# Relative attention: score blocks of 32 queries by four heads, with rounded and remainder query parts stacked

## The reference, cut to what matters

```python
rk2, rv2 = rel_k[idx], rel_v[idx]
attn1 = jnp.einsum('bhqd,bhkd->bhqk', rq, rk)
attn2 = jnp.einsum('bhqd,qkd->bhqk', rq, rk2)
attn = jax.nn.softmax((attn1 + attn2) * (1.0 / math.sqrt(c)), axis=-1)
w1 = jnp.einsum('bhqk,bhkd->bhqd', attn, rv)
w2 = jnp.einsum('bhqk,qkd->bhqd', attn, rv2)
```

## Time and profile before

| | |
|---|---|
| three runs, median (lowest to highest) | 1922.81 us (1922.19 to 1923.03) |
| span of the profiled execution | 1922.3 us, 59270 instructions; its own time around the span is not recorded apart from the runs |
| PE busy in the span | 1656.3 us (86%) |
| VectorE, ScalarE, GpSimd busy | 1402.0 (73%), 938.9 (49%), 882.1 (46%) us |

### The profile page before, as it was taken

One profiled execution on the slowest core, in us unless ns is written; L12 is line 12 of the kernel. 1 busy time (PEld: TensorE's weight loads), 2 busy tenths in 40 slices (PEclk: granted clock), 3 DMA queues, 4 the chain that ended last, 5 costly groups with the idle time before them and its releaser, 6 DMA issues. The chain is left out here.

```text
span 1922.3 us, 59270 instructions
## 1 busy us (share of the span) xinstructions
PE 1656.3 (86%) x21927; PEld 1392.3 (72%) x21927; DVE 1402.0 (73%) x3369; ACT 938.9 (49%) x2305; POOL 882.1 (46%) x1710
## 2 busy tenths in 40 slices
PE   5999999999979884999599999999999999648750
PEld 4888888888858773999478888888888888525430
DVE  6777777877758884666787888888888888635434
ACT  2222212221228770677467777777777777424320
POOL 3333333333202566566232455445555555547771
PEclk9999999999989995999699999999999999869985
DMA  8900000000022001222323333333333333256537
GB/s 298 165 0 0 0 0 0 0 0 0 0 81 102 23 25 55 65 72 65 124 60 63 74 87 78 77 77 78 76 79 80 86 77 78 63 149 171 169 102 271
DMA packets 312667, 147.60 MB, mean 77 GB/s; under 512 B 205238, under 2 KB 291284, under 8 KB 312020
## 3 DMA queue, kind: packets, MB, share of 16 engines
q1 hardware_dynamic: 299876, 118.38, 25.3%
q0 software_dynamic: 12544, 25.91, 3.9%
HBM read 72.03 MB, written 73.37 MB: 76 GB/s over the span
## 5 line engine op out<-in xcount | busy, mean ns | idle before, releaser
L2143 POOL DMA_INDIRECT x_slots<-rel_x,rel_at x128 | 135.5, 1059 | 212.5 <-PE rel_s_ps L1727 186.9
L535 PE MATMUL tok_main_ps<-tok_w_h,tok_feat_h 128*128 128x512 f32 x512 | 205.3, 401 | 0.9 <-DVE tok_feat_low L99 0.9
L1966 ACT ACTIVATE rel_e<-rel_s_ps,rel_neg_max 128x255 f32<-128x255 f32 x512 | 200.2, 482 | 10.7 <-DVE rel_neg_max L2299 9.5
L535 PE MATMUL tok_main_ps<-tok_w_h,tok_feat_l 128*128 128x512 f32 x512 | 200.6, 392 | 0.0
L535 PE MATMUL tok_main_ps<-tok_w_l,tok_feat_h 128*128 128x512 f32 x512 | 200.3, 391 | 0.0
L2299 DVE TENSOR_REDUCE rel_neg_max<-rel_s_ps 128x4 f32<-128x1020 f32 x128 | 155.9, 1218 | 53.2 <-PE rel_s_ps L1727 51.2
L84 POOL TENSOR_TENSOR tok_q_pre<-tok_v_q,tok_v 128x128 f32 (+1 forms) x32 | 39.0, 1219 | 310.5 <-DVE tok_q L274 295.8
L1707 PE MATMUL rel_s_ps<-rel_k_h,rel_q_head_h 128*128 128x256 f32 x512 | 154.6, 302 | 0.2 <-DVE rel_q_head_l L2273 0.2
L1748 PE MATMUL rel_t_ps<-all_k_ident,rel_e 128*128 128x128 f32 x1024 | 139.3, 279 | 14.4 <-issue 14.0
L294 DVE TENSOR_TENSOR tok_prod<-tok_main_ps,tok_v 128x1024 f32<-128x1024 f32 x64 | 78.4, 1225 | 97.9 <-PE tok_main_ps L540 97.9
L1748 PEld LDWEIGHTS rel_t_ps<-all_k_ident,rel_e 128*128 128x128 f32 x1024 | 109.6, 141 | 47.0 <-issue 45.8
(11 more groups left out here) (406 smaller groups left out, 4725.2 us busy)
## 6 DMA issues: line engine op xcount, KB each, us to landing
rel_q_rep<-q_rows SPq DMA_DIRECT2D x256, 64.0 KB, 2.5
o_rows<-rel_rv SPq DMA_DIRECT2D x256, 64.0 KB
x_slots<-early_zeros SPq DMA_DIRECT2D x16, 520.0 KB, 6.2
exp_x<-x_slots SPq DMA_DIRECT2D x32, 260.0 KB, 3.0
y_rows<-early_zeros SPq DMA_DIRECT2D x16, 512.0 KB, 5.8
final_y<-y_rows SPq DMA_DIRECT2D x16, 512.0 KB, 12.0
exp_x<-x_slots SPq DMA_DIRECT2D x72, 65.0 KB, 1.9
q_rows<-rel_qT SPq DMA_DIRECT2D x64, 64.0 KB
```

Source lines behind the costliest of these rows:

```text
L535: nc.tensor.matmul(main_ps[s][:, cols], feat[fk][:, s, j, :], w_p[wk][:, j, cols], start=(j == 0 and (fk, wk) == (0, 0)), stop=False)
L1966: last = nc.scalar.activation(e[u % 2][:, n, 0:L], s_ps[u % 2][:, n, 0:L], ACT.Exp, bias=neg_max[u % 2][:, n:n + 1])
L2143: nc.gpsimd.indirect_dma_start(x1_slots[:], bass.IndirectOffsetOnAxis(ap=at[n][:, k, t:t + 1], axis=0), x1[n][:, t, k, :], None).then_inc( ...
```

## The change

A block of scores becomes 32 queries by four heads. The rounded and the remainder part of a query are stacked along the contraction: four heads by two parts by 16 channels are 128 rows. The key weights and query weights are laid out with each head's channels twice, in two halves a of four heads, so one projection becomes two matmuls. `content` then needs two matmuls per block, one with rounded keys and one with key remainders; the loop puts all rounded-key products of a unit first. The position part takes eight queries by 16 channels as its 128 rows and 32 columns (four heads by eight queries); its table window follows the eight queries. The queries are loaded from DRAM straight into a zeroed `q_pos`, in sixteen loads instead of eight, and `position_queries`, `round_queries`, `queries_rest` and `queries_remainder` are replaced by `split_queries`, one subtraction per head pair and half. The transposed exponentials are copied into `eT` in runs of sixteen, so that `positions` and `values` find a quad's eight heads together.

```diff
-def table_keys(blk):
-    if blk < NBLK // 2:
-        return 0, min(L, BQ * blk + BQ + MAX_REL - 1)
-    return max(0, BQ * blk - MAX_REL + 1), L
+def table_keys(u, q0):
+    if u < NU // 2:
+        return 0, min(L, q0 + OCT + MAX_REL - 1)
+    return max(0, q0 - MAX_REL + 1), L
 def attention_weights(bench, w):
...
-        x, xT, qT = m.sb("x", [P, 2, D]), m.sb("xT", [P, T]), m.sb("qT", [P, T])
+        x, xT, qT = m.sb("x", [P, 2, D]), m.sb("xT", [P, T]), m.sb("qT", [P, 2, OCT, T // OCT])
...
-        q_head = [[m.sb(f"q_head{r}_{k}", [P, T // QUAD, H, QUAD], FP32R) for k in "hl"] for r in range(2)]
-        eT = [m.sb(f"eT{s}", [P, 2, NBLK // 2, P]) for s in range(2)]
-        q_hl = m.sb("q_hl", [P, 2, 2, T], FP32R)
-        q_scale, q_bias, set_up = m.sb("q_scale", [P, 2]), m.sb("q_bias", [P, 2]), m.sem("set_up")
-        q_rep = m.sb("q_rep", [P, H, T // 2])
-        q_pos = [m.sb(f"q_pos{r}", [P, T // (2 * QUAD), H, QUAD]) for r in range(2)]
+        q_head = [[m.sb(f"q_head{r}_{a}", [P, T // OCT, 2, H // 2, QUAD], FP32R) for a in range(2)] for r in range(2)]
+        eT = [m.sb(f"eT{s}", [P, 2, 4, 4, 2, 2, P // 8]) for s in range(2)]
+        q_round = m.sb("q_round", [P, 2, OCT, T // OCT], FP32R)
+        q_scale, q_bias, set_up = m.sb("q_scale", [P, 1]), m.sb("q_bias", [P, 2]), m.sem("set_up")
+        q_pos = [m.sb(f"q_pos{r}", [P, 2, 2, H // 2, QUAD, T // OCT]) for r in range(2)]
...
-        def of_heads(q, k):
-            return q[32 * k:32 * k + 32, :, 2 * k:2 * k + 2, :]
-        def of_pair(part, k):
-            return q_hl[32 * k:32 * k + 32, part].rearrange("p o (g i) -> p g o i", i=QUAD)
-        def keys_for(k, u):
-            return k[:, int(u < NU // 2), :]
+        def by_octets(ap):
+            return ap.rearrange("p (g i) -> p i g", i=OCT)
+        def of_head(ap, a, k):
+            return ap[32 * k:32 * k + 32, a].rearrange("p (w i) g -> p g w i", w=2)
+        def in_blocks(ap):
+            return ap.rearrange("p (a q) (c w k) -> p a (q c w) k", a=2, c=4, w=2)
+        def turned_blocks(eT_t, u):
+            return eT_t[:, 2 * (u % 2):2 * (u % 2) + 2].rearrange("p q c w a k -> p a (q c w) k")
...
                 def repeat_queries(b, r):
...
-                    for f in range(2):
-                        sp.dma_start(q_rows[r][:, f], qT[:].rearrange("p (u f t) -> p u f t", f=2, u=NU)[:, :, f])\
-                            .then_inc(q_out, 16)
-                    sp.wait_ge(q_out, 32 * b + 32)
-                    if after(b, 1):
-                        sp.wait_ge(qp_ready, b)
-                    for f in range(2):
-                        for i in range(QUAD):
-                            at = 64 * f + HD * i
-                            sp.dma_start(q_rep[at:at + HD],
-                                         q_rows[r][:, f].rearrange("(h d) u t -> d h (u t)", d=HD)).then_inc(q_in, 16)
+                    if after(b, 2):
+                        sp.wait_ge(s_done, NU * (b - 1))
+                    sp.dma_start(q_rows[r], qT[:]).then_inc(q_out, 16)
+                    sp.wait_ge(q_out, 16 * b + 16)
+                    if b == 0:
+                        sp.wait_ge(zeroed, 6)
+                    for i in range(OCT):
+                        for a in range(2):
+                            sp.dma_start(q_pos[r][HD * i:HD * i + HD, a, i // QUAD, :, i % QUAD, :],
+                                         q_rows[r].rearrange("(h v d) a i g -> d h v a i g", v=2, d=HD)[:, :, 0, a, i, :])\
+                                .then_inc(q_in, 16)
...
                 def project_k(b):
...
-                    nc.tensor.matmul(pa, wk_sb[:], xT[:], start=True, stop=True).then_inc(k_done, 1)
+                    for a in range(2):
+                        last = nc.tensor.matmul(pa_halves[:, a, :], wk_sb[:, a * P:(a + 1) * P], xT[:], start=True, stop=True)
+                    last.then_inc(k_done, 1)
                 def project_q(b):
...
-                    nc.tensor.matmul(pa, wq_sb[:], xT[:], start=True, stop=True).then_inc(q_done, 1)
+                    for a in range(2):
+                        last = nc.tensor.matmul(pa_halves[:, a, :], wq_sb[:, a * P:(a + 1) * P], xT[:], start=True, stop=True)
+                    last.then_inc(q_done, 1)
...
                 def content(b, u, r):
...
-                        pe.wait_ge(qh_ready, 4 * b + 4)
-                        pe.wait_ge(ql_ready, 4 * b + 4)
-                    for n in range(UB):
-                        blk = UB * u + n
-                        for qk, kk in THREE:
-                            nc.tensor.matmul(s_ps[u % 2][:, n, :],
-                                             q_head[r][qk][:, 4 * blk:4 * blk + 4].rearrange("p c h i -> p (c h i)"),
-                                             keys_for(k_p[r][kk], u),
-                                             start=((qk, kk) == (0, 0) and n % 2 == 0), stop=False,
-                                             skip_group_check=True)
+                        pe.wait_ge(q_split, 2 * b + 2)
+                    for k in range(2):
+                        for q in range(2):
+                            g = 4 * (2 * u + q)
+                            for a in range(2):
+                                nc.tensor.matmul(s_ps[u % 2][:, 2 * a + q, :],
+                                                 q_head[r][a][:, g:g + 4].rearrange("p c w h i -> p (c w h i)"),
+                                                 k_p[r][k][:, a, :], start=(k == 0 and q == 0), stop=False,
+                                                 skip_group_check=True)
                 def position_scores(b, u, r):
...
-                        pe.wait_ge(tables_made, 3)
+                        pe.wait_ge(tables_made, 2)
...
-                        pe.wait_ge(qp_ready, b + 1)
+                        pe.wait_ge(q_in, 16 * 2 * OCT * (b + 1))
...
-                    for k in range(2):
-                        for f in range(2):
-                            n = 2 * f + k
-                            lo, hi = table_keys(UB * u + n)
+                    for q in range(2):
+                        for a in range(2):
...
-                                off = KOFF - BQ * (UB * u + n) - QUAD * c
+                                g = 4 * (2 * u + q) + c
+                                lo, hi = table_keys(u, OCT * g)
+                                off = KOFF - OCT * g
...
-                                    s_ps[u % 2][32 * c:32 * c + 32, n, lo:hi],
-                                    q_pos[r][64 * f:64 * f + 64, 8 * u + 4 * k + c].rearrange("p h i -> p (h i)"),
-                                    table[64 * f:64 * f + 64, off + lo:off + hi], start=False, stop=True,
-                                    skip_group_check=True)
+                                    s_ps[u % 2][32 * c:32 * c + 32, 2 * a + q, lo:hi],
+                                    q_pos[r][:, a, :, :, :, g].rearrange("p w h i -> p (w h i)"),
+                                    table[:, off + lo:off + hi], start=False, stop=True, skip_group_check=True)
                 def turn_e(b, u):
...
-                    if b == 0:
-                        act.wait_ge(tables_made, 1)
-                    for end in range(2):
-                        last = nc.scalar.activation(k_p[r][0][:, end], pa, ACT.Identity, bias=bk_end[:, end:end + 1])
+                    act.wait_ge(set_up, 2)
+                    for a in range(2):
+                        last = nc.scalar.activation(k_p[r][0][:, a], pa_halves[:, a], ACT.Identity, bias=bk_sb[:, a:a + 1])
                 def read_q(b):
...
-                        act.wait_ge(q_out, 32 * b)
-                        act.wait_ge(rest_ready, b)
-                        act.wait_ge(qh_ready, 4 * b)
-                    else:
-                        act.wait_ge(set_up, 2)
-                    for odd in range(2):
-                        nc.scalar.activation(q_hl[:, 0, odd], pa, ACT.Identity, bias=q_bias[:, odd:odd + 1],
-                                             scale=q_scale[:, odd:odd + 1])
-                    nc.scalar.activation(qT[:], pa, ACT.Identity, bias=bq_sb[:], scale=SCALE).then_inc(q_ready, 1)
-                def round_queries(b, r, pairs):
-                    act.wait_ge(q_ready, b + 1)
-                    if after(b, 2):
-                        act.wait_ge(s_done, NU * (b - 1))
-                    act.wait_ge(set_up, 2)
-                    for k in pairs:
-                        nc.scalar.activation(of_heads(q_head[r][0], k), of_pair(0, k).bitcast(FP32), ACT.Copy)\
-                            .then_inc(qh_ready, 1)
+                        act.wait_ge(q_out, 16 * b)
+                        act.wait_ge(q_split, 2 * b)
+                    for a in range(2):
+                        nc.scalar.activation(q_round[:, a], by_octets(pa_halves[:, a]), ACT.Identity, bias=q_bias[:, a:a + 1],
+                                             scale=q_scale[:])
+                    for a in range(2):
```

(56 more changed lines are left out.)

71 lines of the change are left out of this document (31 added, 40 removed).

## The result

The changed kernel takes 2014.59 us (median of four runs, 2008.35 to 2023.0) where the kernel before took 1922.92 in runs beside it (1922.19 to 1926.07): a ratio of 1.0471, 95% interval 1.0443 to 1.05. That is slower, as forecast, but 12 us above the range and 40 above the predicted time.

What follows compares the result with a forecast made beforehand. TensorE was taken to bound slots 0, 1 and 3, ScalarE slot 2, with SP's loop nearly as long. That loop at 24.1 against 22.47 us, over 30 batches, gives 49, plus 3 at the start: 1922.8 + 52 = 1975 us, range 1938 to 2003.

Steps and rivals of the forecast that it cites:

- Rival 1: SP's loop through the query loads and `combine` binds at 24.1 us a batch: +52 us; chance 0.58.
- The size of the loop: From one SP query write through loads, `combine`, projection and `read_q` to the next: 24.1 us a batch.
- 8 x 0.47 us more: In SP's queue, eight additional load issues at the single-issue pace of 0.47 us each: +3.76 us.
- 2.5 us for its landing: Time from issuing the load that feeds `combine` to its arrival, taken from the query loads' median: 2.5 us.
- rival 4: Pauses in SP's queue double with its issues: 24.8 us or more per batch, +77, 2000 us; chance 0.10.
- The last leg: The loop's part from `combine` through maxima, projections and `read_q` to SP's next query write: 6.26 us.
- rival 2: SP's loads stay hidden; only TensorE and ScalarE pay: 0.72 us a batch, +25 us, 1947 us; chance 0.22.
- Rival 3: TensorE's position groups do not slow down: -0.55 us a batch, -13 us, 1910 us; chance 0.06.
- the eight cost at most 3.4: On VectorE, eight half-size subtractions per batch, priced from a 0.43 us copy: at most 3.4 us.
- in slots 0 and 3 under TensorE: VectorE's subtractions, at most 3.4 us, were to be hidden under TensorE's work in slots 0 and 3.
- as long as ScalarE's list: Slot 2 is set by ScalarE's work, not TensorE's; a fourth `read_q` activation adds 0.40 us there.

Runs made afterwards that it cites:

- run 4: The kernel before, with each of its eight query loads split in two of half the heads, same bytes: 2041.37 us, ratio 1.0578.
- run 9: The changed kernel with the eight loads of heads 4 to 7 issued later, behind the turned rows of the batch before; nothing left out: 1981.13 us.
- run 15: The changed kernel, its sixteen loads in one run, with eight subtractions replaced by two of 128 partitions and eight copies: 2014.31 us, ratio 1.0457.
- run 7: The changed kernel with eight of the sixteen loads and only four of the eight subtractions per batch: 1935.59 us, ratio 1.0059.
- run 10: The changed kernel with late loads for heads 4 to 7, and two subtractions of 128 partitions plus eight copies replacing eight subtractions: 1940.45 us.
- run 6: The changed kernel with eight of the sixteen loads and each position product contracting only 64 of its 128 rows: 1978.37 us, ratio 1.0276.
- run 14: The changed kernel with late loads and compact remainder, only the two activations that write rows moved behind slot 2's query rounding: 1934.32 us.
- run 11: The changed kernel with late loads and compact remainder, slot 2 reordered: near positions before query projection, `read_rv` before `read_q`, rows last: 1942.04 us.
- run 12: The kernel before with slot 2 reordered: near positions before query projection, `read_rv` before `read_q`, rows last: 1937.67 us, ratio 1.0082.
- run 1: The changed kernel with its eight subtractions walking elements in another order, source in runs of 32, destination in single strided elements: 2022.22 us.
- run 13: The kernel before, with only the two activations that write rows moved behind the query rounding of slot 2: 1919.77 us, ratio 0.9978.

## Why the prediction was right and wrong

**Direction and mechanism: right.** Rival 1, the likeliest, is what happens: `combine` waits in nearly every batch for a load that stands behind the sixteen. Run 4 shows that doubled issues alone bring this about, run 9 that moving eight of them behind that load ends the wait, and run 15 that relieving VectorE instead gains nothing.

**The size of the loop: wrong, and this is the step that failed.** The prediction put the sixteen loads at 8 x 0.47 us more, 8.26 in all, and "2.5 us for its landing"; the round was to be 24.1. Measured are 8.82 for the loads (0.55 each: the pauses double with the issues, as rival 4 had it), 2.95 from issue to `combine`, and 6.57 instead of 6.26 for the way to the next write. Together 1.32 us a batch, thirty times 39.6 us; 1975 and 40 are the 2015 measured. The single issue was taken from its best case, and the median landing of other loads stood in for the landing of this one. The last leg was summed rightly: in 14 of the 22 rounds it takes 6.26 to 6.35 us. The six rounds above 6.5 are three in which TensorE's clock fell during this leg and three right behind a fall, so what the leg has too much goes with the clock, a term that the prediction put at nothing. Rival 4 priced the issues rightly: its 24.8 us a batch is what the 21 batches without a fall take (24.84). What its 2000 lacks is about the 15 us of the six others.

**TensorE and ScalarE: right.** Content 1.02 us for 1.0, position groups 0.88 and 1.33 for 0.85 and 1.26, query projection 1.06, and `read_q` 1.63 us for 1.65:

```profile
1223.59 1.03 ACT L1950 ACTIVATE rel_q_round<-rel_pa,rel_q_bias,rel_q_scale 128x256 fp32r<-128x256 f32 x2 [0.65 <-PE rel_pa L1697]
1224.51 0.83 ACT L1953 ACTIVATE rel_qT<-rel_pa,attn_bq 128x256 f32<-128x256 f32 x2
1225.22 0.40 ACT L1978 ACTIVATE rel_rv<-rel_t_ps 128x256 f32<-128x256 f32 x1
```

Their sum, rival 2's 23.19 us a batch and 1947 us, is nearly met by runs 7 and 10 (23.02 and 23.07; 1936 and 1940). Part of that is luck: in run 10 slot 0 is 0.26 us longer than before the change, where 0.03 was forecast, and slot 2 only 0.14, where 0.40 was. Rival 3 is refuted: the groups did grow. The Trainium skill, "TensorE: Matmul & The Clock Gate", section "Wait — 56ns, not 53.3ns?", has a floor of about 25 ns between starts. The trace does not agree: the 0.88 us for 32 instructions is 27 ns each, but run 6 has its narrow groups of 64 rows in 0.60 us (median), 19 ns each, so here too the row decides.

**VectorE: wrong, without effect on the time.** That "the eight cost at most 3.4" and lie "in slots 0 and 3 under TensorE" fails on both counts: they take 5.5 us, and in slot 0 the maxima start a full microsecond after the slot (1207.36 against 1206.37). In batch 10 of the kernel before they started 0.14 us after it (1172.04 in the earlier trace rows):

```profile
1172.18 1.22 DVE L2299 TENSOR_REDUCE rel_neg_max<-rel_s_ps 128x4 f32<-128x1020 f32 x1 [0.66 <-PE rel_s_ps L1727]
```

Slots 0 and 1 grew by 1.07 and 0.73 us, where 0.03 and 0.26 were forecast. The price came from a copy with one source; a subtraction with two strided sources is another form. Behind the mended loop this is worth 41 us (run 9 against 10), in front of it nothing (run 15). A forecast of the mended kernel from the same sum would have failed on it.

**Why slot 2 is not ScalarE's alone.** The prediction called slot 2 "as long as ScalarE's list". Run 14 gets a little from shortening that list. Runs 11 and 12 show its other side: two of the list's members lie in SP's loop, and what delays them costs more than the slot gains.

## What to carry to other kernels

When a result returns through a queue that also prefetches, write the loop down with all its legs, take each leg's mean over many rounds rather than the tidiest batch, and look for the leg that waits: here 1.5 us of predicted lengthening was 2.8. Put the load that someone waits for ahead of those needed half a batch later; that one move gave back 33 of 92 us with every load still made. And after removing a limit, measure the next one with the first gone: VectorE's 41 us could not be seen from the changed kernel's time at all. Where a change makes TensorE wait longer, read its granted clock in both kernels before putting the whole difference down to the wait.

## What the runs showed of the hardware

- What a load costs SP's queue does not follow its bytes: 0.60 us an issue for 64 KB (4.79 / 8), 0.55 for 32 KB (run 4) and 0.55 for 8 KB (the change), pauses between issues included.
- A subtraction of 32 partitions by 256 took 682 ns with strided sources and runs of four written, 631 ns with only the destination strided, 416 ns with neither. With 128 partitions and one strided source it took 633 ns, and a copy of 32 by 256 in runs of four 288 ns. So the strides cost time, and four times the partitions did not take longer.
- Position products of 64 rows, eight tiles side by side, took 0.60 and 0.80 us a group in run 6 (medians of slots 1 and 0) where four tiles of 128 rows took 0.88 and 1.33.
- TensorE's granted clock over batches 2 to 29 was 1.00 in the kernel before. It averaged 0.985 in the change, 0.975 in run 1, 0.958 in run 15 and 0.927 in run 4, the runs in which `combine` waits longest. It was 0.994 to 0.997 in runs 11 to 13, and 1.00 in the others. In each fall of the change it went to 0.5 (1.2 GHz) behind an idle stretch of TensorE, and there the `positions` group took 1.71 us instead of 0.92.
